# Flamingo gated block on one core: scores eight units ahead in pairs, one maximum over two PSUM banks a round, and three steps moved

## The reference, cut to what matters

```python
dots = jnp.einsum('bhqd,bhkd->bhqk', q, k) * scale
dots_aux = jnp.einsum('bhqd,bhkd->bhqk', q, ka) * scale
p = jax.nn.softmax(dots, axis=-1)
pa = jax.nn.softmax(dots_aux, axis=-1)
h_main = jnp.einsum('bhqk,bhkd->bhqd', p, v)
h_aux = jnp.einsum('bhqk,bhkd->bhqd', pa, va)
gate = jax.nn.sigmoid(g).reshape(1, H, 1, 1)
out = h_main * (1.0 - gate) + h_aux * gate
...
x = x + jnp.tanh(g_xattn[0]) * _L0_xattn_ref(_layernorm(x, axis=-1), ctx_1024, ...)
x = x + jnp.tanh(g_ffn[0]) * _L0_ffn_ref(_layernorm(x, axis=-1), ...)
```

## Time and profile before

| | us |
|---|---|
| median of 3 runs | 874.03 (873.55 to 874.29) |
| the profiled execution, own time | 874.03 |
| its span, first to last instruction | 872.2 |
| PE busy | 832.4 |
| DVE busy | 690.8 |
| ACT busy | 565.8 |
| POOL busy | 637.7 |

### The profile page before, as it was taken

How to read it: one execution, slowest core, us unless ns; L and a number is a source line. 1 busy time by engine, 2 the same in 40 slices (tenths; PEclk the granted TensorE clock), 3 DMA queues, 4 the chain that set the end, 5 groups by cost and what they waited for, 6 DMA issues and landing times.

```text
span 872.2 us, 20170 instructions
## 1 busy us (share of the span) xinstructions
PE 832.4 (95%) x6733; PEld 646.8 (74%) x6733; DVE 690.8 (79%) x1656; ACT 565.8 (65%) x964; POOL 637.7 (73%) x602
## 2 busy tenths in 40 slices
PE   5899999998898889999999999999999999999997
PEld 3467777776675668888888888887888888888885
DVE  6789899998888858778777877967976977877655
ACT  4377888887777756566566567548557556656554
POOL 2476888887883357887787786887787788778785
PEclk9999999999999999999999999999999999999999
DMA  5567777777653156646554654654746555655552
GB/s 131 175 173 188 182 192 189 186 193 182 168 156 81 32 138 151 151 119 148 134 134 123 168 133 109 169 129 110 179 119 143 145 134 126 148 131 140 143 137 58
DMA packets 113747, 125.27 MB, mean 144 GB/s; under 512 B 28000, under 2 KB 76064, under 8 KB 112208
## 3 DMA queue, kind: packets, MB, share of 16 engines
q1 hardware_dynamic: 110768, 123.47, 56.8%
q10 hardware_dynamic: 2880, 0.59, 0.4%
HBM read 103.55 MB, written 19.96 MB: 142 GB/s over the span
## 4 chain that ended last, share of the span: by engine, by line
PE 75%; DMA 6%; DVE 2%; issue 2%; ACT 2%; POOL 1%; SPq 0%; DVEq 0%; ACTq 0%; POOLq 0%
PE bank L1963 20%; PE bank L1965 20%; PE bank L1964 20%; PE bank L1305 4%; DMA stack_q<-nmaxT 3%; PE bank L1292 3%; PE bank L1279 2%; DMA stack_k<-k_scratch 1%; PE bank L1261 1%; PE bank L1249 1%; DMA cwb<-wts_scratch 1%; ACT prob L787 1%; PE bank L1313 1%; PE bank L1940 1%; PE bank L1326 1%
## 5 line engine op out<-in xcount | busy, mean ns | idle before, releaser
L1640 POOL TENSOR_TENSOR hid<-act,cwb 128x512 f32<-128x512 f32 x264 | 424.4, 1616 | 125.7 <-DVE act L1867 71.7
L1693 ACT ACTIVATE silu<-bank 128x512 f32<-128x512 f32 x256 | 152.8, 597 | 193.7 <-PE bank L1965 189.2
L1867 DVE TENSOR_TENSOR act<-silu,bank 128x512 f32<-128x512 f32 (+1 forms) x264 | 180.5, 684 | 118.8 <-ACT silu L1693 76.6
L1963 PE MATMUL bank<-xhi,weights_hi 128*128 128x512 f32 x520 | 206.7, 397 | 0.4 <-ACT silu L1693 0.4
L1875 DVE TENSOR_TENSOR hlo<-hid,hhi 128x512 fp32r<-128x512 f32 x256 | 199.4, 779 | 7.3 <-ACT hhi L1699 7.0
L1965 PE MATMUL bank<-xlo,weights_hi 128*128 128x512 f32 x520 | 204.1, 392 | 0.0
L1964 PE MATMUL bank<-xhi,weights_lo 128*128 128x512 f32 x520 | 203.8, 392 | 0.0
L984 DVE TENSOR_REDUCE mx<-bank 128x4 f32<-128x512 f32 x256 | 167.5, 686 | 22.4 <-PE bank L1279 18.7
L1699 ACT ACTIVATE hhi<-hid 128x512 fp32r<-128x512 f32 (+1 forms) x264 | 165.0, 625 | 13.3 <-POOL hid L1640 10.9
L787 ACT ACTIVATE prob<-bank 128x1024 f32<-128x1024 f32 x128 | 131.0, 1024 | 64.0 <-PE bank L1292 61.8
L1965 PEld LDWEIGHTS bank<-xlo,weights_hi 128*128 128x128 f32 x520 | 97.6, 188 | 22.0
(11 more groups left out here) (235 smaller groups left out, 1003.0 us busy)
## 6 DMA issues: line engine op xcount, KB each, us to landing
cwb<-wts_scratch SPq DMA_DIRECT2D x174, 384.0 KB, 5.4
stack_k<-k_scratch SPq DMA_DIRECT2D x30, 384.0 KB
k_scratch<-parts_k SPq DMA_DIRECT2D x15, 384.0 KB, 3.3
stack_q<-q_scratch SPq DMA_DIRECT2D x30, 192.0 KB
k_scratch<-parts_k SPq DMA_DIRECT2D x15, 256.0 KB, 3.9
q_scratch<-parts_q SPq DMA_DIRECT2D x15, 192.0 KB, 2.2
xin<-in_x_dram SPq DMA_DIRECT2D x16, 128.0 KB, 2.5
cin<-in_ctx_dram SPq DMA_DIRECT2D x16, 128.0 KB, 2.6
```

What stands on the lines that cost most here:

```text
L1640: pool.tensor_tensor(h_buf[k][:], a_buf[k][:], cwb[slot][:, q % GP, :], ALU.mult).then_inc(h_ok, 1)
L1693: act.activation(s_buf[k % RS][:], g_bank[k % 2][:], ACT.Silu).then_inc(s_ok, 1)
L1867: nc.vector.tensor_tensor(a_buf[k % RS][at], s_buf[k % RS][at], u_bank[k % 3][at], ALU.mult).then_inc(a_ok, 1)
L1963: nc.tensor.matmul(bank, w[0], mh, start=first, stop=False)
```

## The change

The first pass now runs eight units ahead, so that round r of batch b holds both units of round r of batch b+2 (`S_HEAD` is turned by one to keep the halves opposite). DVE takes one maximum a round, over both banks (`two_banks`), where it took one for each bank; `mx_ok` counts rounds. PE waits once a round, for the maximum of the round before, and may then write either bank. `minus_max` moves behind the fourth maximum of a batch, and `turn_max` ahead of the projections of round 0. `evac_nmax` moves behind the first maximum, and `shift_rows` on ACT from round 1 to round 0, ahead of `high_of` (except near the end, `late`). `residual(b-2)` stands behind the first maximum of a batch where `residual(b-1)` stood at its end. Ahead of the loop, all eight units of batch 1 are now done, and `minus_max(1)`.

```diff
@@
-S_HEAD = (10, 12, 14, 0, 2, 4, 6, 8)
+S_HEAD = (8, 10, 12, 14, 0, 2, 4, 6)
 LAG = 2
-AHEAD = 7
@@
                 b, n, i, odd = BODY * g + k, 2 * g + k // CH, k // CH, k % CH
                 first = b == 0
                 more = not (last and i == 1)
+                late = last or (before_last and k == BODY - 1)
                 for r in range(ROUNDS):
                     exps(b, r)
-                    if r == 1 and not (last and k == BODY - 1):
-                        shift_rows(b + 1)
                     if r == 0 and not first:
                         copy_o(b - 1, 1 - odd)
+                    if r == (1 if late else 0) and not (last and k == BODY - 1):
+                        shift_rows(b + 1)
@@
                                               ALU.subtract, ALU.mult)
             ins.then_inc(xn_ok, 1)
 
-        def maxima(b, par, u):
-            wait(dve, s_mm, UNITS * b + u + 1)
-            if u == 0:
+        def maxima(b, par, r):
+            wait(dve, s_mm, UNITS * b + 2 * r + 2)
+            if r == 0:
                 wait(dve, nm_ok, b - 1)
-            f, h = S_HEAD[u] // HH, S_HEAD[u] % HH
-            nc.vector.tensor_reduce(mx[par][:, 2 * f:2 * f + 2, h:h + 2].rearrange("p a h -> p h a"),
-                                    s_bank[u % 2][:].rearrange("p (h a k) -> p h a k", h=2, a=2),
+            f, h = S_HEAD[2 * r] // HH, S_HEAD[2 * r] % HH
+            nc.vector.tensor_reduce(mx[par][:, 2 * f:2 * f + 2, h:h + 4].rearrange("p a h -> p h a"),
+                                    two_banks[:].rearrange("p (h a k) -> p h a k", h=4, a=2),
                                     AXX, ALU.max).then_inc(mx_ok, 1)
 
         def minus_max(b, par, turned):
-            wait(dve, mx_ok, UNITS * (b + 1))
+            wait(dve, mx_ok, ROUNDS * (b + 1))
             wait(dve, nm_mm, b)
             wait(dve, t_ev, turned)
             nc.vector.tensor_scalar(neg, mx[par][:], -1.0, None, ALU.mult).then_inc(nm_neg, 1)
@@
         gate_consts()
         split(1, 1, 1, 0)
         split(1, 1, 1, 1)
-        for u in range(UNITS):
-            maxima(0, 0, u)
+        for r in range(ROUNDS):
+            maxima(0, 0, r)
         minus_max(0, 0, 3)
         evac_nmax(0)
-        for u in range(AHEAD):
-            maxima(1, 1, u)
-            if u == 4:
+        for r in range(ROUNDS):
+            maxima(1, 1, r)
+            if r == 2:
                 copy_ka(2)
+        minus_max(1, 1, 3)
 
         def body(g, left):
             last = left == 0
@@
                 b, n, i, odd = BODY * g + k, 2 * g + k // CH, k // CH, k % CH
                 first = b == 0
                 one_more, two_more = not (last and k == BODY - 1), not (last and k >= BODY - 2)
+                late = last or (left == 1 and k == BODY - 1)
                 for u in range(UNITS):
-                    if u + AHEAD < UNITS:
-                        if one_more:
-                            maxima(b + 1, 1 - odd, u + AHEAD)
-                    elif two_more:
-                        maxima(b + 2, odd, u + AHEAD - UNITS)
-                    if u == UNITS - AHEAD - 1 and one_more:
-                        if b == NB - 2:
-                            dve.wait_ge(fe_ok, 1)
-                        minus_max(b + 1, 1 - odd, min(n + 3 + odd, NC))
-                    if u == 1 and one_more:
+                    if u == 0 and b == NB - 2:
+                        dve.wait_ge(fe_ok, 1)
+                        minus_max(NB - 1, 1, NC)
+                    if two_more and u % 2 == 0:
+                        maxima(b + 2, odd, u // 2)
+                    if u == (1 if late else 0) and one_more:
                         evac_nmax(b + 1)
+                    if u == 1 and b > 1:
+                        residual(b - 2, (b - 2) // CH, (b - 2) // CH % 2, odd)
+                    if u == 7 and two_more and b + 2 < NB - 1:
+                        minus_max(b + 2, odd, min(n + 4, NC))
                     if u == 1 and first:
                         norm_sums(3)
                         norm_mean(3)
@@
                         copy_ka(n + 3)
                     if u == 5 and not odd and n + 4 < NC:
                         norm_sums(n + 4)
-                    if u == 7 and not first:
-                        residual(b - 1, *((n, i, 0) if odd else (n - 1, 1 - i, 1)))
+                    if u == 7 and b == NB - 1:
+                        residual(b - 1, n, i, 0)
                     if u == 7 and not odd and n + 4 < NC:
                         norm_mean(n + 4)
                     if left == 1 and (k, u) in STATS_AT:
@@
         def scores(b, u, j):
             n, c, s = b // CH, b % CH, b // CH % NST
             h = S_HEAD[u] + j
-            if (c == 0 or n == 0) and j == 0 and u in (0, 3):
+            if (c == 0 or n == 0) and j == 0 and u in (0, 4):
                 if n == 0:
                     wait(pe, stk0[h // HH][c], 32)
                 else:
                     wait(pe, stk[h // HH][s], 32 * ((n - 1) // NST + 1 if s else n // NST))
             if u == 0 and j == 0:
                 wait(pe, shift_zero, CH if n == NST else b - CH * NST + 1)
-            if j == 0:
-                wait(pe, mx_ok, UNITS * b + u - 1)
+            if j == 0 and u % 2 == 0:
+                wait(pe, mx_ok, ROUNDS * b + u // 2)
             at = slice(*SCORE_ROWS[h // HH])
             ins = nc.tensor.matmul(s_bank[u % 2][:, j * TC:(j + 1) * TC], q_of(n)[at, h % HH, c, :],
                                    k_of(n)[at, h % HH, c].rearrange("p a t -> p (a t)"), start=True, stop=True)
@@
         pe.wait_ge(v_ev, 1)
         project_qk(2, 0)
         turn_max(0)
-        for u in range(AHEAD):
+        for u in range(UNITS):
             scores(1, u, 0)
             scores(1, u, 1)
             if u == 3:
@@
                 late = last or (before_last and k == BODY - 1)
                 for r in range(ROUNDS):
                     for u in (2 * r, 2 * r + 1):
-                        if u + AHEAD < UNITS:
-                            ahead = (b + 1, u + AHEAD) if one_more else None
-                        else:
-                            ahead = (b + 2, u + AHEAD - UNITS) if two_more else None
+                        ahead = (b + 2, u) if two_more else None
                         shifted(b, u, 0)
                         if ahead:
                             scores(*ahead, 0)
@@
                             weighted(b, odd, u - LAG, n, i)
                         elif not first:
                             weighted(b - 1, 1 - odd, u + UNITS - LAG, n if odd else n - 1, i if odd else 1 - i)
+                    if r == 0 and one_more and not late:
+                        wait(pe, nm_ev, b + 1)
+                        turn_max(b + 1)
                     if r == 0 and odd and n + 3 < NC:
                         wait(pe, v_ev, n + 2)
                         project_qk(n + 3, 1 - i)
@@
                         wait(pe, ka_ev, min(n + 3, NC))
                         project_v(n + 1, (i + 1) % 2, 0)
                         project_v(n + 1, (i + 1) % 2, 1)
-                    if r == 0 and one_more and not late:
-                        wait(pe, nm_ev, b + 1)
-                        turn_max(b + 1)
                     if r == 3 and not first:
                         out_proj(b - 1, 1 - odd)
                     if before_last and k == 3 and r == 2:
```

More of the change, by code:

```diff
@@ L173, in attention @@
 def attention(nc, sem, m, m_cw, psum, v):
-    wide = v["wide"]
+    wide, two_banks = v["wide"], v["two_banks"]
     x, ctx, x2d, q_d, k_d = v["x"], v["ctx"], v["x2d"], v["q_d"], v["k_d"]
```

2 lines of the change are left out of this document (1 added, 1 removed).

## The result

The changed kernel took 883.19 us in the median of 4 runs (881.36 to 883.76) against 873.79 for the kernel before in the same session, a ratio of 1.011 with a 95% interval of 1.0083 to 1.0137. It is slower, by 9.4 us where the forecast had 7.6. Its profiled execution took 881.36 us, 7.33 more than that of before (874.03).

The account below looks back on a forecast made before the run. Two close limits bound an attention chunk: the engines' rounds (PE and ACT ring, DVE close) and the stack_k supply. Opening +3.1, then +4.0, -0.2 and +0.7 gave +7.6 on 874.03: 881.6 us, own range 879 to 885, 8-in-10 range 874.8 to 886.0.

Parts of the forecast that it names:

- The issue on ACT: Round 0, batches 4 to 25: the transfer's issue blocks ACT 0.62 us, delaying weights_hi and the second exponential by 0.23 us.
- The floor of a round from the pair: Every loop round lasts at least 1.91 us, with a 1.20 us maximum: round 1 +0.14, round 3 +0.06.
- it takes the place of DVE's 0.14: Round 1: ACT's +0.23 us replaces the pair's +0.14 instead of adding, as both run beside each other.
- The supply: Loop chunks: the stack_k chain grows 1.1 us over two chunks, 0.56 a chunk, nearly the same as the engines' limit.
- The earlier transfer: Chunk starts: maxima's transfer issued 0.86 us earlier, so waits should go; gains 1.3 us each at batches 22 and 24.
- The opening: Ahead of the loop: PE and DVE alternate over pairs instead of overlapping, starting the supply chain 3.1 us later.
- Moved at no cost: turn_max ahead of the projections and copy_ka one maximum later in the opening cost nothing; residual's new place costs nothing either.
- The end: Batches 26 to 31, without the moved transfer in the last: +0.7 us.
- the issue doesn't block: Rival, ACT: the transfer's 0.62 us hides under osb and weights_hi; +4.2 us, 878.2 us; chance 0.2.
- supply and transfers decide: Rival, loop and opening: engines' extra time fills transfer waits, only the transfer's gain is left; -5 us, 869; chance 0.13.
- gain and loss cancel: Rival, whole kernel: the opening costs its 3.1 us and the loop gains 3; 874 us; chance 0.08.
- The slow clock: Rival, opening: PE stays at 1.2 GHz for eight more rounds; +5 us, 887 us; chance 0.09.

Follow-up runs that it names:

- e5: The changed kernel again, unaltered, as yardstick for the timed runs; 883.56 us, ratio 1.0126 to the kernel before.
- e1: The changed kernel with the issue of shift_rows behind high_of (weights_hi) in round 0 on ACT; 880.96 us, ratio 1.0097 to the kernel before.
- e4: The changed kernel with one maximum per bank everywhere and the issue of shift_rows behind weights_hi; 874.09 us, ratio 1.0020 to the kernel before.
- e6: The changed kernel with one maximum per bank everywhere, the issue of shift_rows still ahead of weights_hi; 878.14 us, ratio 1.0077 to the kernel before.
- e8: The changed kernel with the issue of shift_rows back in round 1 of ACT for all batches; 883.82 us, ratio 1.0136 to the kernel before.
- e3: The changed kernel with the issue behind weights_hi and one maximum per bank for batches 0 and 1; 877.68 us, ratio 1.0044 to the kernel before.
- e2: The changed kernel with one maximum per bank for batches 0 and 1 only, pairs kept in the loop; 877.98 us, ratio 1.0061 to the kernel before.
- e7: The changed kernel with the residual at its old place on DVE; 883.56 us, ratio 1.0138 to the kernel before.
- e10: The changed kernel with the residual at its old place in the last four batches; 881.85 us, ratio 1.0088 to the kernel before.
- e11: e4 with the residual at its old place everywhere; 872.58 us, ratio 0.9989 to the kernel before.

## Why the prediction was right, term by term

| term | predicted | measured | again, in e5 |
|---|---|---|---|
| opening, to batch 2 | +3.1 | +3.15 | +3.04 |
| batches 2 to 18 | +4.0 | +4.26 | +5.74 |
| batches 18 to 26 | -0.2 | -0.76 | -1.39 |
| batches 26 to 31 | +0.7 | +0.66 | +0.68 |
| sum | +7.6 | +7.31 at batch 31, +7.33 in time | +8.07 at batch 31, +8.25 in time |

The two largest causes were seen rightly, the issue on ACT and the pairs in the opening. That each term also came out so closely is in part luck: inside most of them, parts that were too large or missing cancel.

- **The issue on ACT: right, and shown** by e1, e4 against e6, and e8. Its term was mis-sized only little: 0.20 and 0.22 a batch where I took 0.23. The rounds show it; the medians of the pairs that differ in the issue's place alone say 2.2 us (e1), 0.3 (e3 against e2), 4.0 (e6 against e4) and none (e8).
- **The floor of a round from the pair: wrong in place, and too dear.** I took 1.20 us for the reduction; it is 1.225. The Trainium skill, VectorE: DVE Perf Modes, The TRN2 errata, gives 1.19 by its formula, an estimate; the measured row stands 0.03 above it. I put +0.14 in round 1 and +0.06 in round 3. But a round's start waits for the exponential, not for the maximum. The wait comes inside the next round, ahead of its scores. In e1, where ACT's part is gone, round 0 is 0.11 longer than before and round 2 of even batches 0.17: 0.39 a chunk; I had 0.40. But e4, with single maxima, keeps 0.12 of it in its rounds 0, so the pairs cost 0.27 and the rest belongs to something that I had put at nothing. The size was hit by luck. In the odd batch round 2 is long for other work and hides the wait. So "it takes the place of DVE's 0.14" was right only for round 2: round 0 pays on top.
- **The supply: not what decided.** The chunk's engine rounds give 16.54 and the chunks took 16.63. I trusted 16.65 because both limits gave it; only one was at work. POOL's waits ahead of `weights_lo` rose from 35.9 to 39.8 us, and loads of `stack_k` held PE for 0.39 us in batch 6 and for 2.04 in batch 20, and a weight load of PE for 0.38 in batch 8.
- **The earlier transfer: the waits went, but its place on ACT is not shown to be why.** The waits at batches 20, 22 and 24 went, and at 20 `stack_k` took its place (2.04 us). Before, rounds 3 of batches 19, 21 and 23 took 3.34, 3.17 and 3.15 us instead of 1.85, 4.1 too many; four longer chunks cost 2.6 and `stack_k` 0.9 more than before, which leaves about the measured gain. In e8, with the issue back in round 1, these waits stay away too: whether the loads of `stack_k` stand ahead of the transfer changes with the pace of the whole loop, and no run separates that from the earlier copy of `nmaxT`.
- **The opening: the sum right, two parts off.** Pairs cost 4.7 there, and the rest of the change gains 1.5 (e2). I had 3.1 for the pairs and nothing for the rest; the earlier `turn_max`, which I had put at no cost, is one candidate for the gain.
- **"Moved at no cost": half right.** `residual` costs nothing in its new place in the loop, and spares the issue 0.1 to 0.2 us a batch there (e7). In batch 31 it makes a round 0.85 us longer, which I had not looked at, but 0.13 of that reach the experts, and all of it lies behind the stretch of the table.
- **The end: the sum right by two parts that cancel.** Before, batch 28 also started with a wait of 1.19 us for the transfer of the maxima (271.50), which I had not counted and which is gone. The rounds of batches 26 to 30 are some 1.8 us longer for it, and 1.1 of that is paid back by round 3 of batch 27 (2.32 us instead of 3.43).

Of the rivals, "the issue doesn't block" is refuted by e1; "supply and transfers decide" and "gain and loss cancel" by the rounds. The slow clock did last longer in the opening: the last `scores` matmul of 0.39 us or more starts at 45.29 us, before at 41.64, and from 45.67 and 43.47 on they take 0.27; but that lies inside the +3.1, of which it may be a part. The profiled execution was the fastest of its four runs, and the median of the others, 883.4, is 1.8 us above the forecast. What makes them longer was not profiled.

## What to carry to other kernels

A reduction over two banks saves instructions on an engine that has room, and takes away the overlap by which the matmuls wrote one bank while the other was read; the price appears where the writer next needs a bank, not in the round of the reduction. When a transfer's issue is moved on a computing engine, look at what stands behind it: 0.62 us of issue is free beside a running instruction or an idle wait, and on the path ahead of one that the next stage needs. Before a step that is late for nobody is moved, see who waits for it in the last batches, where other work stands in between. And when two terms of a sum come out as forecast, take them apart all the same: here a run with one of the parts alone showed that the sum was right and the parts were not.

## What the runs showed that I had not expected

**The clock fell within or behind attention in four of the thirteen profiled executions:** in e2 from 273.7 to 277.1 us and from 304.5 to 314.7, in e8 from 304.1 to 314.4, in e10 from 212.3 to 215.7 and in e11 from 202.2 to 205.6. The two of e2, with what stood ahead of them; columns: stretch, length, busy time (instructions) of PE, PEld, DVE, ACT and POOL, granted clock, DMA share, GB/s:

```profile
271.00:273.70 2.70, 1.53 (x28) 1.00 (x23) 1.92 (x6) 1.55 (x3) 2.42 (x4) 1.00 0.51 103
273.70:277.10 3.40, 3.40 (x34) 2.71 (x34) 1.23 (x1) 2.02 (x3) 3.02 (x5) 0.50 0.00 0
...
300.00:304.00 4.00, 2.78 (x40) 1.91 (x38) 3.69 (x30) 3.62 (x7) 1.97 (x2) 1.00 0.01 2
304.00:314.00 10.00, 9.70 (x93) 6.70 (x94) 5.63 (x31) 4.58 (x8) 1.78 (x3) 0.52 0.10 27
```

PE was busy 1.53 us of 2.7 around its wait of 1.17 us at batch 28, and 2.78 of 4 around its wait of 0.98 us in batch 31; each time it then stood at the lower level, 1.2 GHz. Sixteen `weighted` matmuls took 0.98 us instead of 0.64, the first matmul of the experts came 12.4 us behind the start of batch 31 instead of 9.0, and from there to the end 579.9 us passed where e1, e3 and e4 took 577. In e8 it was the same (12.5 and 580.2). In e10 and e11 the fall came with waits of 1.26 and 1.39 us for `stack_k` in batch 20, whose round 0 took 5.07 and 5.27 us where e5's took 3.82. The changed kernel, e1, e3 to e6 had the wait in batch 31 and no fall behind it, and the kernel before waited 1.51 us at batch 20 without one, so such a wait alone does not decide. Of e2's twelve executions the four with a mean clock of 0.992 to 0.996 took 879.8 to 883.7 us, and the others 876.6 to 879.4. That fits falls as a part of the spread, some 3.4 us for a long one, but only one of the twelve was profiled.

**The recorded clock of the opening can be missing.** The changed kernel's two profiled executions, first and e5:

```profile
22.00:30.00 8.00, 3.95 (x18) 1.70 (x17) 4.73 (x6) 3.80 (x6) 3.69 (x9) 1.00 0.67 201
```

```profile
22.00:30.00 8.00, 3.94 (x20) 1.75 (x18) 4.82 (x7) 3.83 (x6) 3.69 (x9) 0.71 0.55 161
```

One records 1.00 and the other 0.71, and PE's busy time is the same. But the matmuls say more than the busy time. The same four `scores` matmuls, first and e5:

```profile
24.72 1.03 PE L1281 MATMUL bank<-stack_k,stack_q 52*128 52x256 bf16 x4 [1.32 <-DVE mx L984]
```

```profile
24.52 0.61 PE L1281 MATMUL bank<-stack_k,stack_q 52*128 52x256 bf16 x4 [1.32 <-DVE mx L984]
```

By these lengths (0.42 us a matmul, and 0.27) the first execution ran there at the lower level, 1.2 GHz, while its record says 1.00, and e5 ran at 2.4 GHz. e5's record agrees with its matmuls: 1.00 from 22.8 to 26.2 us, where they take 0.27, and 0.50 from 26.2 on, where they take 0.42 again. So a record of 1.00 in the opening is to be checked against the length of a known matmul, and that is why means of 0.98 and 1.00 stand beside equal times: the first trace has no record of its low stretch, which lasts to about 45.6 us.
